# Preparing two turns of a feed-forward stage inside the attention stage ahead of it, and regrouping its turns from five groups to four

## What is computed

```python
# dequantize(w, s, z): (w - z) * s, with z and s shared by each 128 input rows
gate = silu(x @ dequantize(gate_w, gate_s, gate_z))      # 512 -> 1792
up   = x @ dequantize(up_w, up_s, up_z)                  # 512 -> 1792
out  = (gate * up) @ dequantize(down_w, down_s, down_z)  # 1792 -> 512
```

## Time and profile before

| | us |
|---|---|
| median of 3 runs | 1651.47 (1648.33 to 1655.12) |
| the profiled execution | 1650.77, its span 1649.0 |
| cross-attention stage, its last DVE instruction | begins at 526.7 |
| feed-forward stage, first instruction | 528.4 |
| its last matmul of lines 1645 and 1646 | begins at 730.9 |
| the stage's last DVE instruction | begins at 754.3 |
| next stage, first DMA issue | 755.9 |

### The profile page before, as it was taken

The page is one execution under the profiler, slowest core; times in us unless marked ns, Lnnn a source line. Parts: engine busy times, 40 slices in busy tenths (PEclk is TensorE's granted clock), DMA queues, the critical chain, the costliest instruction groups (busy, mean ns, idle before and its releaser), DMA issues. The chain is left out here.

```text
span 1649.0 us, 29540 instructions
## 1 busy us (share of the span) xinstructions
PE 1552.9 (94%) x10984; PEld 1290.7 (78%) x10984; DVE 951.0 (58%) x1693; ACT 798.9 (48%) x2426; POOL 768.0 (47%) x624
## 2 busy tenths in 40 slices
PE   6999999999998779998999889999999999999997
PEld 4777888888886557876777678888888888888875
DVE  3947503333356777778677835555555555555656
ACT  3342324444443445445988734454455445445532
POOL 3403215343321779763533527655455545554413
PEclk9999999999999899999999999999999999999999
DMA  6100200010101743204000021201101011010001
GB/s 211 39 1 1 58 20 21 21 38 5 53 1 46 230 134 128 90 1 122 1 2 27 27 91 39 65 26 39 35 31 52 17 49 39 27 33 14 1 1 51
DMA packets 61777, 77.84 MB, mean 47 GB/s; under 512 B 12168, under 2 KB 41348, under 8 KB 61636
## 3 DMA queue, kind: packets, MB, share of 16 engines
q1 hardware_dynamic: 61172, 74.63, 14.4%
q0 software_dynamic: 464, 1.32, 0.3%
HBM read 73.85 MB, written 2.10 MB: 46 GB/s over the span
## 5 line engine op out<-in xcount | busy, mean ns | idle before, releaser
L1152 POOL TENSOR_TENSOR xa_rs<-xa_ms,minus_half 128x5 f32<-128x5 f32 x64 | 74.8, 1168 | 160.5 <-DVE xa_ms L1423 160.3
L1158 POOL TENSOR_TENSOR xa_prob<-xa_prob,xa_inv 128x512 f32<-128x512 f32 x64 | 66.7, 1042 | 139.0 <-DVE xa_inv L1390 139.0
L766 POOL TENSOR_TENSOR xa_prob<-xa_prob,xa_inv 128x1024 f32<-128x1024 f32 x32 | 60.7, 1895 | 140.8 <-DVE xa_inv L1029 140.8
L1418 DVE TENSOR_REDUCE xa_ssq<-pre 128x4 f32<-128x512 f32 x64 | 43.9, 686 | 134.4 <-ACT pre L1354 134.4
L1368 ACT ACTIVATE xa_prob<-xa_prob,xa_peak 128x128 f32<-128x128 f32 x256 | 99.7, 391 | 41.9 <-DVE xa_peak L1434 41.9
L101 PE MATMUL late_bank<-late_q_hi,xT_hi 128*128 128x512 f32 x284 | 117.9, 415 | 0.0
L1745 DVE SCALAR_TENSOR_TENSOR ff_acc<-ff_ring,ff_sT,ff_acc 128x512 f32<-128x512 f32 x140 | 100.6, 747 | 21.1 <-ACT ff_acc L1699 14.5
L103 PE MATMUL late_bank<-late_q_lo,xT_hi 128*128 128x512 f32 x284 | 112.6, 397 | 0.0
L102 PE MATMUL late_bank<-late_q_hi,xT_lo 128*128 128x512 f32 x284 | 112.5, 396 | 0.0
L1354 ACT ACTIVATE pre<-late_bank 128x512 f32<-128x512 f32 x64 | 38.2, 597 | 141.3 <-PE late_bank L103 141.3
L1985 POOL TENSOR_TENSOR pre<-pre,sa_inv 128x1024 f32<-128x1024 f32 x32 | 63.7, 1989 | 92.0 <-DVE sa_inv L2192 92.0
(11 more groups left out here) (414 smaller groups left out, 4929.9 us busy)
## 6 DMA issues: line engine op xcount, KB each, us to landing
pre<-in_wq SPq DMA_DIRECT2D x8, 1024.0 KB, 5.7
late_raw_o<-in_wo SPq DMA_DIRECT2D x8, 1024.0 KB, 5.3
ff_dn_q<-in_down_w SPq DMA_DIRECT2D x7, 512.0 KB, 3.9
ff_dn_z<-in_down_z SPq DMA_DIRECT2D x7, 512.0 KB, 5.0
ff_dn_s<-in_down_s SPq DMA_DIRECT2D x7, 512.0 KB, 5.8
pre<-in_wq SPq DMA_DIRECT2D x16, 192.0 KB, 3.4
pre<-in_wo SPq DMA_DIRECT2D x16, 192.0 KB, 3.8
pre<-in_xT SPq DMA_DIRECT2D x4, 512.0 KB, 8.1
```

The source lines that it names most:

```text
L766: pool.tensor_tensor(prob[:, t % 3, :, :], prob[:, t % 3, :, :], bc(inv[:, t % 3, :], 2, [P, Q, KEYS]), ALU.mult).then_inc(s["norm"], 1)
L1152: pool.tensor_tensor(rs[:, :], ms[:, :], m.minus_half[:, 0:Q + 1], ALU.pow).then_inc(s["rs"], 1)
L1158: pool.tensor_tensor(prob[:, u % 2, :, :], prob[:, u % 2, :, :], bc(inv[:, u % 2, :], 2, [P, Q, S]), ALU.mult).then_inc(s["norm"], 1)
```

## The change

1. **Turns 0 and 1 are prepared in the cross-attention stage.** Their gate and up weights live in two buffers (`early_w`) that both stages can see. They are subtracted there on DVE, two pieces behind each of the steps t = 24, 25 (turn 0) and 27, 28 (turn 1); the first piece of a turn waits for its transfer. The down slice of turn 0 is subtracted on DVE in step 30 and multiplied on POOL in step 31, in one instruction of 128x1024 each. SP loads turn 0, waits for its 4 pieces, loads turn 1, waits, and loads the down slice of turn 0, all through `m.pre`. To make room, some buffers of the cross-attention stage (parts of its wide key, value, query and output weights) lie in `early_w`; their contents and the instructions on them stay.
2. **The feed-forward stage starts without them.** Of turn 0 only `down_high` on ACT (unit 0) and `down_low` on POOL (unit 1) are left in it. Its weights of turns 2 to 6 and down slices of turns 1 to 6 stand at new units.
3. **SP issues the down slice of a turn before the gate and up slice of the turn two later.**
4. **Groups**: (0,1), (2,3), (4,5), (6) in place of (0), (1,2), (3,4), (5), (6), which is 4, 4, 4, 2 tiles. There are 8 half blocks, not 10, and 32 `out_rows`, not 40; the number of matmuls is the same, since a row block of 4 tiles has 12.

```diff
+    WEIGHTS_AT = ((24, 24, 25, 25), (27, 27, 28, 28))
+    DOWN_AT = 30
...
-                ffn_stage_inputs(sp, io, *ffn_stage_buffer(m.pre), 0, s["ld_next"])
-                sp.wait_ge(s["ld_next"], 96)
+                for T in range(2):
+                    if T:
+                        sp.wait_ge(s["w"], KC * T)
+                    ffn_stage_inputs(sp, io, *ffn_stage_buffer(m.pre), T, s["ld_w"])
+                sp.wait_ge(s["w"], KC * 2)
+                dn_q, dn_z, dn_s = ffn_down_buffer(m.pre)
+                ffn_down_inputs(sp, io, dn_q.bitcast(INT32), dn_z.bitcast(INT32), dn_s, 0, s["ld_w"])
+                sp.wait_ge(s["ld_next"], 32)
+                sp.wait_ge(s["ld_w"], 64 * 2 + 48)
...
+                    if t == DOWN_AT + 1:
+                        pool.wait_ge(s["dn_sub"], 1)
+                        w, _, scale = ffn_down_buffer(m.pre)
+                        pool.tensor_tensor(w, w, scale, ALU.mult)
...
+                    for T in range(2):
+                        for c in range(KC):
+                            if WEIGHTS_AT[T][c] == t:
+                                weights(T, c)
+                    if t == DOWN_AT:
+                        dve.wait_ge(s["ld_w"], 64 * 2 + 48)
+                        q, z, _ = ffn_down_buffer(m.pre)
+                        dve.tensor_tensor(q, q.bitcast(INT32), z.bitcast(INT32), ALU.subtract).then_inc(s["dn_sub"], 1)
...
-GROUPS = ((0,), (1, 2), (3, 4), (5,), (6,))
+GROUPS = ((0, 1), (2, 3), (4, 5), (6,))
...
-        mid = {3: [0, 1], 4: [2, 3], 5: [4, 5], 6: [6], 7: [7], **{n: [n - 1] for n in range(9, 22)}, 22: [22], 23: [24, 25], 24: [26, 27],
-               25: [28, 29], 26: [30, 31], 27: [32, 33]}
-        end = {21: [21], 22: [23], 27: [34, 35]}
+        mid = {**{n: [n - 5] for n in range(5, 25)}, 25: [20, 21], 26: [22, 23], 27: [24, 25]}
+        end = {27: [26, 27]}
...
-        weight_units = {1: (1, 2, 2, 2), 2: (4, 4, 5, 5), ...
-        down_units = {0: (1, 1, 1, 2, 2, 2), 1: (3, 3, 4, 5, 5, 6), 2: (6, 6, 7, 7, 7, 8), ...
+        weight_units = {2: (4, 5, 5, 6), 3: (7, 8, 8, 9), 4: (10, 11, 12, 13), 5: (14, 15, 16, 17), 6: (18, 19, 20, 21)}
+        down_units = {0: (None, None, None, 0, 1, 1), 1: (3, 3, 3, 4, 4, 4), 2: (6, 6, 7, 8, 8, 8), ...
...
+                ffn_stage_inputs(sp, io, *stage[0], 2, s["ld_even"])
+                for T in range(1, TURNS):
+                    if T >= 2:
+                        sp.wait_ge(s["dn_sub"], T - 1)
+                        sp.wait_ge(s["dn_w"], MT * (T - 1))
+                    ffn_down_inputs(sp, io, dn_q[:, :, :], dn_z[:, :, :], dn_s[:, :, :], T, s["ld_dn"])
+                    if T + 2 < TURNS:
+                        if T == 1:
+                            sp.wait_ge(s["dn_lo"], MT)
+                        else:
+                            sp.wait_ge(s["w"], KC * (T - 1))
+                        ffn_stage_inputs(sp, io, *stage[T % 2], T + 2, s["ld_odd" if T % 2 else "ld_even"])
```

More of the change, by code:

```diff
@@ L52, in __init__ @@
         self.norm_bank = None
+class Early:
+    def __init__(self, sb):
+        self.w = [sb(f"early_w{n}", [P, KC * 2 * WIDE], F32R) for n in range(2)]
 class Late:
@@ L649, in cross0_stage, with pieces @@
         SLOT = KC * FEATS
+        def pieces(flat):
+            return [flat[:, n:n + FEATS] for n in range(0, flat.shape[1], FEATS)]
         raw_k, raw_v = (m.pre[:, n * SLOT:(n + 1) * SLOT].rearrange("p (c n) -> p c n", c=KC) for n in range(2))
@@ L1005, in _, with weights @@
                 dve.wait_ge(n0["x"], B)
+                def weights(T, c):
+                    q, z = ffn_stage_buffer(m.pre)
+                    if c == 0:
+                        dve.wait_ge(s["ld_w"], 64 * (T + 1))
+                        if T == 0:
+                            dve.wait_ge(s["q_mm"], 3 * B)
+                        else:
+                            dve.wait_ge(s["rows"], 3 * B)
+                    dve.tensor_tensor(ffn_weights(m.early.w[T])[:, c, :, :], q[:, c, :, :], z[:, c, :, :], ALU.subtract).then_inc(s["w"], 1)
                 for t in range(STEPS):
@@ L1474, in ffn_stage_buffer, with ffn_weights, ffn_down_buffer, ffn_down_inputs @@
     return [flat[:, n * KC * 2 * WIDE:(n + 1) * KC * 2 * WIDE].bitcast(INT32).rearrange("p (c a n) -> p c a n", c=KC, a=2) for n in range(2)]
+def ffn_weights(flat):
+    return flat[:, :].rearrange("p (c a n) -> p c a n", c=KC, a=2)
+def ffn_down_buffer(flat):
+    return [flat[:, n * MT * D:(n + 1) * MT * D].rearrange("p (k n) -> p k n", k=MT) for n in range(3)]
+def ffn_down_inputs(sp, io, q, z, scale, T, done):
+    part = slice(T * MT, (T + 1) * MT)
+    sp.dma_start(q, io["down_w"].rearrange("(m p) n -> p m n", p=P)[:, part, :]).then_inc(done, 16)
+    sp.dma_start(z, io["down_z"][part, :].partition_broadcast(P)).then_inc(done, 16)
+    sp.dma_start(scale, io["down_s"][part, :].partition_broadcast(P)).then_inc(done, 16)
 def ffn_scales(sp, io, dest, done):
@@ L1503, in ffn0_stage @@
         other = sb("other", [P, 2 * KC * 2 * WIDE])
-        stage = [ffn_stage_buffer(m.pre), ffn_stage_buffer(other)]
-        w = sb("w", [P, 3, KC, 2, WIDE], F32R)
+        stage = [ffn_stage_buffer(other), ffn_stage_buffer(m.pre)]
+        first_down = ffn_down_buffer(m.pre)[0]
+        w = [ffn_weights(x) for x in (*m.early.w, sb("w", [P, KC * 2 * WIDE], F32R))]
         sT = sb("sT", [P, 2, KC, TILES])
@@ L1673, in _ @@
                     hb, k = TABLE[n]
[L1674 to L1675 removed]
+                    if turn_of(n) >= 2 and hb % 2 == 0 and k % MT == 0:
+                        pe.wait_ge(s["w"], KC * (turn_of(n) - 1))
                     for i in range(4):
[L1677 to L1678 removed]
                         group(n, i)
@@ L1767, in add_rows @@
                     dve.tensor_tensor(m.xtok[:, b, :], m.xtok[:, b, :], rows[r % 2][:, :], ALU.add).then_inc(s["add"], 1)
-                q, z = stage[0]
-                for c in range(KC):
-                    dve.tensor_tensor(w[:, 0, c, :, :], q[:, c, :, :], z[:, c, :, :], ALU.subtract).then_inc(s["w_first"], 1)
                 dve.wait_ge(s["sT"], 1)
@@ L1777, in _ @@
                     part(n, 3)
-                    for T in range(1, TURNS):
+                    for T in range(2, TURNS):
                         for c in range(KC):
@@ L2368, in program @@
         m.scales, m.own = sb("scales", [P, P]), sb("own", [P, HC])
+        pair = ExitStack()
         for n, stage in enumerate(STAGES):
             used = []
+            if n == PAIRED[0]:
+                m.early = Early(lambda name, shape, dt: pair.enter_context(nc.sbuf_tensor(name, shape, dt)))
             if n == SHARED:
@@ L2379, in program @@
             stage(nc, m, io, sem)
+            if n == PAIRED[1]:
+                pair.close()
             if n < len(STAGES) - 1:
```

71 lines of the change are left out of this document (28 added, 43 removed).

## The result

| | before | after |
|---|---|---|
| median of 5 runs each, us | 1648.33 (1646.74 to 1655.12) | 1640.54 (1639.57 to 1641.55) |
| ratio, 95% interval | | 0.9949 (0.9932 to 0.9966) |
| the profiled execution, its span | 1650.77, 1649.0 | 1641.55, 1639.8 |
| feed-forward stage, first DMA issue to the next stage's first | 528.4 to 755.9: 227.5 | 529.6 to 746.5: 216.8 |
| first matmul into the ring to the end of unit 27 | 529.17 to 731.3: 202.1 | 530.18 to 721.7: 191.5 |

The kernel became faster by 7.8 us, on the edge of the 0.5% that the prediction set as the boundary between faster and the same: 0.47% by the medians, 0.51% by the ratio, whose interval reaches from 0.34 to 0.68% faster. So it is faster for certain, by about half a percent. Profile against profile the difference is 9.2: the feed-forward stage gave 10.7, and the work outside it took back 1.5.

The account below looks back on a forecast made before the run. PE was taken to bound the feed-forward stage only from 614 on, with POOL's list next at its start. 1650.77 - 9.7 (feed-forward) + 0.4 (cross-attention) = 1641.5 us; own range 1638.5 to 1645, overall range 1637 to 1650.

Parts of the forecast that it names:

- What bounds, and where the gain is: Feed-forward stage: PE bounds it only from 614 on; 24.5 us lost, behind turn 1's transfer and POOL's low parts.
- The gate: Feed-forward unit 5: PE's first row block waits for POOL's low parts of turns 0 and 1, until 561.8.
- 18 instructions of 1.26: POOL's list from product(0) to the first row block: 22.7 us of work, without its waits.
- From the gate on: First row block to end of unit 27: 672 matmuls take 157.2 us, plus 1.6 and 1.0, ending at 721.6.
- The lower clock: PE behind its wait at the first row block: matmuls run slower, costing 1.6 us, bounds 0 and 3.2.
- The cross-check: PE at 564.5 in the feed-forward stage: some 97 to 99 matmuls done, against 91 recorded before.
- Cross-attention: Cross-attention stage: the moved preparation costs 0.4 us, 0.1 from step 28 and 0.3 from step 30; bounds 0 and 12.3.
- Rival 1: Feed-forward stage before 614: all PE's lost time goes except the cold start's 1.4, giving 1628.0; chance 0.05.
- Rival 2: Later feed-forward units: stalls behind POOL's low parts or ACT return, 6.1 and 4.1 stay lost, up to 1651.7; chance 0.22.
- Rival 3: Cross-attention tail: POOL keeps the port for normalization and multiplication, scaling(4) is 2.5 later, giving 1644.0; chance 0.08.
- Rival 4: Cross-attention stage: moved work is exposed, up to 12.3 us, giving 1653.4, slower than before; chance 0.06.
- The signs: Profile after: first row block 561 to 563, no DVE DMA wait in units 0 to 3, barrier 528.4 plus 0 to 1.

Follow-up runs that it names:

- experiment 3: Changed kernel with early preparation kept, but the old five groups and unit tables restored; median 1645.54 us, ratio 0.9979 to the kernel before.
- experiment 4: Kernel before with only the four groups and their tables, and all four weight pieces of turn 1 in unit 1; median 1646.08 us, ratio 0.9978 to before.
- Experiment 1: Changed kernel with POOL's two low parts of turn 0's down slice done twice; 1644.43 us.
- experiment 6: Changed kernel with down work of turns 0 and 1 moved from POOL to DVE and ACT rounding turn 1's slice ahead of high(3); 1638.52 us in one run.
- experiment 7: Changed kernel with down work of turns 0 and 1 moved to DVE and ACT's part 4 ahead of high(n-1) in units 1 to 5; 1638.62 us.
- Experiment 8: Changed kernel with each of the eight moved weight pieces done twice on DVE in the cross-attention stage; 1641.85 us.
- experiment 2: Changed kernel with the second low part of turn 2's down slice in unit 9, not 8; 1642.06 us in one run.
- experiment 5: Changed kernel with ACT evacuating part 4 ahead of high(n-1) in units 1 to 5; first to last ring matmul 190.8 us, against 191.3.

## Why the prediction held, point by point

- **What bounds, and where the gain is.** Held. The wait for the transfer and the wait of `down(2)` are both gone, the first stretch kept its loss, and the second and third gave the gain. Experiments 3 and 4 show each stall by itself. What the prediction took as given, that no row block stands before unit 5, is a choice of the new groups, and experiment 3 shows its price in the first stretch (13.0 lost, against 5.4 with the old groups).
- **The gate.** The mechanism held, its size was short: it came 34.1 us behind the first ring matmul, forecast 32.6 (561.8 - 529.17). product(0) began 7.9 us behind that matmul, as forecast (537.1 - 529.17). From there to POOL's last low part it is 26.1, forecast 24.7. POOL's waits were 2.26 (forecast 2.0). The rest is the term "18 instructions of 1.26": total(3) took 2.26 and one product 1.72, each while DVE worked from SBUF to SBUF (the down subtraction at 551.45, a weight piece at 556.69). Together these two are 1.4 us over their usual 1.28, of the 2.3 that the prediction had in its upper bound ("each piece holds POOL for its length"). PE came to the gate at 562.6, not 559, since it had stood for ACT; POOL was later still. Experiment 1 shows that the gate passes on what is put in it; experiments 6 and 7, that it yields only as far as DVE allows.
- **From the gate on.** 672 matmuls was a miscount. The row blocks of `end` stand behind the last ring matmul, so 748 matmuls, not 760, lie in the stretch, before as after, and 660 behind the gate; the note that six had no record was wrong with it, and so was the loss before, which is 202.1 - 748 x 0.234 = 27.1, not 24.5. Behind the gate 157.2 should have been 154.4 (660 x 0.234). The lower clock took 1.9 (forecast 1.6): the first nine matmuls of the row block lasted 4.0 us, 2.1 at full pace. All else took 1.0. Measured from 564.2 to 721.5: 157.3, forecast 159.8. The miscount of 2.8 more than hid the gate's 1.5: the stretch was to shrink by 9.7 and shrank by 10.4 to 10.6. That the two errors went opposite ways is luck.
- **The cross-check** of 97 to 99 matmuls at 564.5 failed. At 564.2, just ahead of the gate, 88 had started (the row's x90 counts two filler products); with the offset of 1.0 us in the start, the moment to compare is 565.5, and by then it was 91, where it had been 90 before. The later gate explains a part of it. The check was also too high by the prediction's own terms: 88 at 561.8 and then 2.7 us at 0.43 us each make 94.
- **Cross-attention.** 0.4 forecast, 0.06 found; step 28 went as described (maximum 1.1 late, exponentials not at all). What I let through in step 30 was absorbed. Experiment 8 shows how much room there is. The 8.5 us that I called the most a transfer takes in the earlier trace rows is the median of three; DVE has no wait for a transfer in the feed-forward stage after all the same.
- **What fell out.** Rival 1: the first row block at 564.3, not before 558; the first stretch still loses 13 us. Rival 2: no such wait in the trace; its mechanism is real (experiments 2 and 3), its price was 2.3 us for the one turn of experiment 2 and 4.05 + 2.7 for that of experiment 3, where I had given both stretches 10.2. Rival 3: the multiplication on POOL began at 508.34, as the normalization ended, and took 2.58; the scaling took 1.92 (before 2.11) and ended at 508.67, 0.28 behind the end of the normalization, before 0.29. So the second instruction on POOL didn't hold the waiting one on DVE. The rule of the Trainium skill, "SBUF — State Buffer", "Who interferes with whom", that of two such instructions the first one keeps the port pair for its whole length, agrees with the 1.92, where a scaling without POOL beside it took 0.55. It agrees, too, with the first pair of pieces (449.33), for which the prediction had 0.4 more by it: 1.61 us, 0.33 over the 1.28 of the pairs that met nothing on POOL. Rival 4: excluded, 0.06 against 9.7.
- **The total.** 1641.5 forecast for the profiled execution, 1641.55 measured. That closeness is luck: 0.9 more gain in the stretch and 0.3 less cost were offset by 1.5 us in stages that the change doesn't touch. Between medians of five runs the gain was 7.8, since the execution profiled before (1650.77) stood 2.4 over the median of the five, and the one after 1.0 over its own.
- **The signs.** The row block was to start at 561 to 563 and started at 564.26; the barrier was to come at 528.4 plus 0 to 1, and the first DMA issue behind it came at 529.62. The first stage's offset of 1.2 us accounts for nearly all of both. The other signs came as stated.

## What to carry to other kernels

A stage whose engine mix is unbalanced at its start isn't mended by taking away the longest wait: write down each engine's list up to the first point that needs it all, and the longest list is the new gate. Joining groups can move that point onto more work, as here from turn 0's low parts to those of turns 0 and 1: look at each half of a change by itself, and stretch by stretch. Preparation moved into the stage ahead cost next to nothing here, since the engine that waits for the delayed result had two instructions of its own first; the way to know is to double the moved work. Where a buffer is passed between two engines, put its last reader a full unit ahead of its next writer: one unit in a table was 2.3 us.

## What the runs showed of the hardware

- DVE and POOL on SBUF at once slow each other in both directions: a pair of DVE subtractions or products of 128x512 took 1.28 us where POOL did nothing (the pieces at 485.46) and 3.32 to 3.45 among POOL's instructions in experiment 6; POOL's sum of 128x512 took 2.26 instead of 1.28 beside one 1.27 us piece of DVE. (The pieces at 485.46 read integers, the pairs of experiment 6 floats; no run has the same pair both ways.) Work moved from POOL to DVE thus grew from 7.6 to 9.2 us.
- PE waited 2.47 us, did four matmuls, waited 1.61 and then ran slow: matmuls 0.63 and then 0.40 apiece in the records, 0.43 and 0.23 from start to start, with the granted clock at 0.92 in that stretch: partly at 1.2 GHz. In experiment 5 the waiting was one piece of 4.6 us, and 13 matmuls behind the gate were slow, where the changed kernel had 9 and experiment 8, with the same stage, 7. A part of the difference lies ahead of the gate: there the changed kernel ran two matmuls slow between its two waits, and experiment 8 four, which cost nothing, since POOL's low part was later anyway. In experiment 1 it was 10 behind 2.09 us, in experiment 3 it was 13 behind 4.05.
- Stages that the kernels share differ from one execution to the next. The first DMA issue of the feed-forward stage comes at 527.76 to 529.92 in the seven profiles with the same code up to there (after, experiments 1 to 3 and 5 to 7), and the part behind the stage takes 891.7 us (experiment 2) to 895.2 (experiment 3). For gains of a few us the stage's own interval tells more than the total.
